# Half-target edge buckets: count matmuls of 314 columns, four plain evacuations on ScalarE, and biases added later

## The reference

```python
u = xn @ root + bias
for r in range(8):
    mask = (edge_type == r)
    sums = segment_sum(xn[src] * mask[:, None], dst, num_segments=625)
    cnt = segment_sum(mask, dst, num_segments=625)
    u = u + (sums / maximum(cnt, 1)[:, None]) @ weight[r]
z = concatenate([u, xn], 1) @ w_gate + b_gate
h = tanh(u) * z + xn * (1 - z)
```

## Time and profile before

| | us |
|---|---|
| median of 3 runs | 1880.09 |
| lowest, highest | 1879.5, 1880.28 |
| profiled execution: span from first to last instruction | 1878.8 |
| PE busy (share of the span) | 1794.9 (96%) |
| DVE busy | 1023.3 (54%) |
| ACT busy | 478.5 (25%) |
| POOL busy | 701.1 (37%) |
| chain that ended last: share of PE | 84% |

### The profile page before, as it was taken

One profiled execution on the slowest core, in us unless ns is written; L12 is line 12 of the kernel. 1 busy time (PEld: TensorE's weight loads), 2 busy tenths in 40 slices (PEclk: granted clock), 3 DMA queues, 4 the chain that ended last, 5 costly groups with the idle time before them and its releaser, 6 DMA issues.

```text
span 1878.8 us, 28666 instructions
## 1 busy us (share of the span) xinstructions
PE 1794.9 (96%) x9953; PEld 1477.4 (79%) x9953; DVE 1023.3 (54%) x2540; ACT 478.5 (25%) x1055; POOL 701.1 (37%) x609
## 2 busy tenths in 40 slices
PE   6999999999999999999999999954999999999999
PEld 4876689987777778787777887742899888878987
DVE  7888999997254543526354356786632224362311
ACT  3139956662010110101011145243100000111100
POOL 2110000003634435353534444200485552345862
PEclk9999999999999999999999999956999999999999
DMA  4532222224213121231313534110354351113322
GB/s 134 154 109 77 73 86 79 75 67 129 91 38 89 45 72 56 66 86 47 94 33 113 172 84 131 45 46 7 96 164 146 104 156 51 37 55 118 90 73 66
DMA packets 129282, 162.23 MB, mean 86 GB/s; under 512 B 14288, under 2 KB 75368, under 8 KB 128922
## 3 DMA queue, kind: packets, MB, share of 16 engines
q1 hardware_dynamic: 100848, 120.93, 21.5%
q10 hardware_dynamic: 22250, 23.53, 4.0%
q0 software_dynamic: 6080, 16.40, 2.9%
HBM read 135.51 MB, written 25.30 MB: 86 GB/s over the span
## 4 chain that ended last, share of the span: by engine, by line
PE 84%; DVE 6%; ACT 6%; issue 1%; DVEq 1%; DMA 1%; POOL 0%; ACTq 0%; SPq 0%
PE ps L367 22%; PE ps L368 22%; PE ps L369 21%; PE ps L1236 9%; PE ps L892 3%; ACT sc_col L838 2%; ACT sc_row L837 1%; PE ps L1201 1%; DVE w_lo L318 1%; PE ps L881 1%; PE ps L1156 1%; DMA nat<-in_x 1%; ACT w_hi L313 1%; PE ps L1183 1%; PE ps L1211 0%
## 5 line engine op out<-in xcount | busy, mean ns | idle before, releaser
L367 PE MATMUL ps<-w_hi,xt_hi 128*125 128x512 f32 x1320 | 539.0, 408 | 9.1 <-DVE xt_lo L549 3.5
L256 POOL TENSOR_TENSOR w_hi<-w_stage,zero 128x512 fp32r<-128x512 f32 x256 | 276.8, 1081 | 684.4 <-PE ps L369 670.0
L368 PE MATMUL ps<-w_lo,xt_hi 128*125 128x512 f32 x1320 | 523.0, 396 | 0.0
L369 PE MATMUL ps<-w_hi,xt_lo 128*125 128x512 f32 x1320 | 521.5, 395 | 0.0
L259 POOL TENSOR_TENSOR w_lo<-w_stage,w_hi 128x512 fp32r<-128x512 f32 x256 | 346.2, 1352 | 20.1
L367 PEld LDWEIGHTS ps<-w_hi,xt_hi 128*125 128x125 f32 x1320 | 246.6, 187 | 67.1 <-DVE xt_lo L549 4.3
L369 PEld LDWEIGHTS ps<-w_hi,xt_lo 128*125 128x125 f32 x1320 | 246.0, 186 | 63.3
L368 PEld LDWEIGHTS ps<-w_lo,xt_hi 128*125 128x125 f32 x1320 | 246.3, 187 | 53.5
L367 PE MATMUL ps<-xt_hi,w_hi 128*128 128x314 f32 x736 | 250.5, 340 | 1.3 <-DVE ring L2430 0.6
L369 PE MATMUL ps<-xt_hi,w_lo 128*128 128x314 f32 x736 | 225.9, 307 | 0.0
L368 PE MATMUL ps<-xt_lo,w_hi 128*128 128x314 f32 x736 | 225.7, 307 | 0.0
(11 more groups left out here) (392 smaller groups left out, 2390.2 us busy)
## 6 DMA issues: line engine op xcount, KB each, us to landing
w_stage<-in_stream SPq DMA_DIRECT2D x374, 256.0 KB, 2.7
pre<-ring POOLq DMA_DIRECT2D x30, 250.0 KB, 3.8
a_qt<-pre_t SPq DMA_DIRECT2D x18, 312.5 KB, 3.8
a_qt<-pre_t ACTq DMA_DIRECT2D x14, 312.5 KB
pre_t<-ring_t POOLq DMA_DIRECT2D x12, 312.5 KB, 2.8
...
```

Of the source, the lines that this page charges most:

```text
L256: POOL.tensor_tensor(w_hi[:, q, :], w_stage[:, q % NST, :], zero[:].to_broadcast([128, 512]), ALU.add).then_inc(S("hi_done"), 1)
L367: PE.matmul(dst, l_hi, r_hi, start=first, stop=False)
L368: PE.matmul(dst, l_hi, r_lo, start=False, stop=False)
L369: return PE.matmul(dst, l_lo, r_hi, start=False, stop=last)
```

## The change

**Buckets.** The key becomes (type x 5 + tile) x 2 + (target is 314 or more): 80 buckets, each padded to whole chunks of 128, again 240 chunks. The column one-hot has 314 columns instead of 626; each chunk's counts are one matmul of 314 columns in a bank of its own, with no sum over two chunks. ACT copies two chunks in one instruction; DVE adds each chunk apart (240 adds of 314). The row one-hots of four chunks are made by one tensor-tensor comparison of 512 elements (`iota1_by4` against four columns of `slot_row`), and PE reads each with a step of four elements. Addresses are ready-made in `g_start` and loaded into four registers at once. The one-hot of chunk c + 4 stands behind the add of chunk c.

**Sorting.** `key_hot` has 28 rows; three fields of 8 bits share a row, with weights 1, 2^8, 2^16, and a scan over 28 x 166 elements counts all 84. `ranks` and `rank_fields` take each edge's rank out of the packed sums; `positions` makes each bucket's start by 80 comparisons with a multiply, in int16, and folds them.

**Evacuations and biases.** Groups 0 to 3 leave PSUM by ACT without bias (`evacuate_plain`). Their biases are loaded by SP (`load_bias_h`) and added by DVE (`bias_half`) to nat, which has relations' u by then, and to z before its first use.

```diff
-GROUP = 256
-NGROUP = (EDGES + NBUCKET * (GROUP - 1)) // GROUP
-NCHUNK = 2 * NGROUP
+SPLIT = 314
+NKEY = 2 * NBUCKET
+FIELDS, NROW = 3, 28
+NFIELD = FIELDS * NROW
+CHUNK = 128
...
+        def evacuate_plain(g):
+            for m in range(T):
+                wait_bank(ALE, g, m, c0, g0)
+                if g:
+                    ALE.wait_ge(S(f"st{tag}_{m}"), 16 * g)
+                ALE.activation(ring[:, m, :], ps[0:P, m, :], ACT.Copy).then_inc(S("bank_free"), 1)
...
         def evacuate(g):
-            DVE.wait_ge(S("b" + tag), 16 * g + 16)
+            DVE.wait_ge(S("b" + tag), 16 * (g - G_PLAIN) + 16)
             for m in range(T):
                 wait_bank(DVE, g, m, c0, g0)
-                if g:
-                    DVE.wait_ge(S(f"st{tag}_{m}"), 16 * g)
+                DVE.wait_ge(S(f"st{tag}_{m}"), 16 * g)
...
+        DVE.tensor_tensor(key_hot[:], e_row[:].unsqueeze(1).to_broadcast([P, NROW, EW]),
+                          iota16[0:P, 0:NROW].unsqueeze(2).to_broadcast([P, NROW, EW]), ALU.is_equal)
+        split_low_dve(8, 11)
+        DVE.drain()
+        DVE.tensor_tensor(key_weight[:], key_hot[:], e_weight[:].unsqueeze(1).to_broadcast([P, NROW, EW]), ALU.mult)
         split_low_dve(11, 16)
...
+        kw = key_weight[:].rearrange("p b c -> p (b c)")
+        DVE.tensor_tensor_scan(scan[:].rearrange("p b c -> p (b c)"), kw, kw, 0.0, ALU.add, ALU.max)
...
+    def ranks():
+        DVE.tensor_tensor(scan[:], scan[:], key_hot[:], ALU.mult)
+        DVE.drain()
+        n = NROW
+        while n % 2 == 0:
+            n //= 2
+            DVE.tensor_tensor(scan[:, 0:n], scan[:, 0:n], scan[:, n:2 * n], ALU.add)
+            DVE.drain()
+        DVE.tensor_reduce(e_rank[:], scan[:, 0:n].rearrange("p b c -> p c b"), AX.X, ALU.add)
+        DVE.drain()
...
+    def positions():
+        for b in range(NKEY):
+            DVE.tensor_scalar(key_start[:, b, :], e_key16[:], float(b), b_off[:, b:b + 1], ALU.is_equal, ALU.mult)
+            if b == NKEY // 2:
+                split_low_dve(24, 27)
         split_low_dve(27, 31)
         DVE.drain()
-        n = NBUCKET
+        n = NKEY
         while n % 2 == 0:
             n //= 2
-            if 2 * n == NBUCKET:
-                h = n // 2
-                DVE.tensor_tensor(scan[:, 0:h], scan[:, 0:h], scan[:, n:n + h], ALU.add)
-                evacuate(2)
-                DVE.tensor_tensor(scan[:, h:n], scan[:, h:n], scan[:, n + h:2 * n], ALU.add)
+            DVE.tensor_tensor(key_start[:, 0:n], key_start[:, 0:n], key_start[:, n:2 * n], ALU.add)
+            if 2 * n == NKEY:
                 split_low_dve(31, 32)
...
-        DVE.tensor_reduce(e_pos[:], scan[:, 0:n].rearrange("p b c -> p c b"), AX.X, ALU.add)
+        DVE.tensor_reduce(e_pos[:], key_start[:, 0:n, 0:EC].rearrange("p b c -> p c b"), AX.X, ALU.add)
+        DVE.drain()
+        DVE.tensor_tensor(e_pos[:], e_pos[:], e_rank[:, 0:EC], ALU.add)
...
+    LEAD_HOT, STARTS = 4, 4
+    def pair_bank(g):
+        return 4 if g % 2 else 6
+    def hist_hot(c):
+        if c % 4 == 0:
+            if c >= 8:
+                DVE.wait_ge(S("hi_pe"), c - 4)
+            DVE.tensor_tensor(hot_row[c // 4 % 2][:], iota1_by4[:],
+                              slot_row[:, c:c + 4].unsqueeze(1).to_broadcast([128, 128, 4]), ALU.is_equal)
+        if c >= 8:
+            DVE.wait_ge(S("hi_pe"), c - 7)
+        DVE.tensor_scalar(hot_col[c % 8][:], iota1_16[:, 0:SPLIT], slot_col[:, bass.ds(c, 1)], None,
+                          ALU.is_equal).then_inc(S("hi_dve"), 1)
+    def hist_copy(g):
+        b = pair_bank(g)
+        ALE.wait_ge(S("hi_pe"), 2 * g + 2)
+        if g >= 4:
+            ALE.wait_ge(S("hi_add"), 2 * g - 6)
+        ALE.activation(counts[g % 4][:], ps[0:P, b:b + 2, 0:SPLIT], ACT.Copy).then_inc(S("hi_main"), 1)
+    def hist_starts(c):
...
+    def hist_add(c, start):
+        DVE.wait_ge(S("hi_main"), c // 2 + 1)
+        if c:
+            DVE.wait_ge(S("hi_add"), c)
+        o = adj[:, bass.ds(start, SPLIT)]
+        DVE.tensor_tensor(o, o, counts[c // 2 % 4][:, c % 2, :], ALU.add).then_inc(S("hi_add"), 1)
+    def hist_pe(g):
+        if g >= 2:
+            PE.wait_ge(S("hi_main"), g - 1)
+        if g == 1:
+            PE.wait_ge(S("bank_free"), (SC0 + SC_GROUPS + 1) * T)
         for j in range(2):
-            q = 2 * gm + j
...
+            c = 2 * g + j
+            PE.wait_ge(S("hi_dve"), c + 1)
+            PE.matmul(ps[0:P, pair_bank(g) + j, 0:SPLIT], hot_row[c // 4 % 2][:, 0:P, c % 4], hot_col[c % 8][:],
+                      start=True, stop=True).then_inc(S("hi_pe"), 1)
...
+        mk = bucket_counts()
         split_low_dve(16, 21)
+        ranks()
         dense(1)
         mk = bucket_sums(mk)
-        evacuate(1)
         split_low_dve(21, 24)
-        mk = group_buckets(mk)
+        rank_fields()
+        mk = chunk_buckets(mk)
         dense(2)
         mk = pack_buckets(mk)
-        positions(evacuate)
+        positions()
         mk = packed_buckets(mk)
         ALE.dma_start(bias_t[:].rearrange("p g b -> p (g b)"), a["bias"][B_PRE0 + 4:B_PRE0 + 8, :].rearrange(
...
-            for c in range((g + 1) * KT, (g + 2) * KT):
+            for c in range((g + 1) * KT, (g + 2) * KT - 1):
                 split_act(c)
-        load_bias(3)
+            evacuate_plain(g)
+            split_act((g + 2) * KT - 1)
         for c in range(C_HAND, C_HAND + 4):
             split_act(c)
         wait(ALE, mk)
-        mk_zero = sig(ALE.activation(adj[:].bitcast(F32), zero[0:P, :].to_broadcast([P, NBUCKET * NB // 2]), ACT.Copy), "act_step")
+        mk_zero = sig(ALE.activation(adj[:].bitcast(F32), zero[0:P, :].to_broadcast([P, NBUCKET * NB // 2 + 1]), ACT.Copy), "act_step")
...
                 DVE.wait_ge(S("sc_pe"), sc_per + EC + 1)
-                DVE.tensor_copy(slot[:, :, 0:NCHUNK], slot_ps.rearrange("p (a c) -> p a c", a=2))
+                DVE.tensor_copy(slot_col[:], slot_ps[:, 0:NCHUNK])
+                DVE.tensor_copy(slot_row[:], slot_ps[:, NCHUNK:2 * NCHUNK])
                 DVE.drain()
-                for n in range(2):
-                    hist_dve_hot(n, n)
+                for c in range(LEAD_HOT):
...
+        starts = dict(enumerate(hist_starts(0)))
         for h in range(HI_GROUPS):
             for n in range(per):
-                g = h * per + n
-                if g + 2 < NGROUP:
-                    hist_dve_hot(g + 2, (g + 2) % 4)
-                if chunk_at(h, n):
-                    split_dve(chunk_at(h, n))
-                if g % 4 == 0:
-                    packed = DVE.value_load(gpack[0:1, g // 4:g // 4 + 1], min_val=0, max_val=2 ** 24 - 1)
-                hist_dve_add(g, g % 4, packed)
+                for c in (2 * (h * per + n), 2 * (h * per + n) + 1):
+                    hist_add(c, starts[c])
+                    if c + LEAD_HOT < NCHUNK:
+                        hist_hot(c + LEAD_HOT)
+                    if c % STARTS == 0 and c + STARTS < NCHUNK:
+                        starts.update(zip(range(c + STARTS, c + 2 * STARTS), hist_starts(c + STARTS)))
...
+    def load_bias_h(row):
+        for g in range(2):
+            r = B_PRE0 + row + g
+            SP.dma_start(bias_h[g][:], a["bias"][r:r + 1, :].rearrange("o (k f) -> o k f", k=4).to_broadcast([P, 4, 128])).then_inc(S("ld_bh"), 16)
...
         if c == C_PROJ + 4:
             SP.dma_start(bias_p[:], a["bias"][B_PROJ0:B_PROJ0 + 2, :].rearrange("(o g) f -> o g f", o=1).to_broadcast(
                 [P, 2, 512])).then_inc(S("ld_bp"), 16)
+            SP.wait_ge(S("a0_C"), REL)
+            load_bias_h(0)
+        if c == C_GATE + 1:
+            SP.wait_ge(S("gsum"), 1)
+            load_bias_h(2)
         if c == C_GATE + 4:
...
+    def bias_half(into, g):
+        into_g = into[:, :, g * 512:(g + 1) * 512].rearrange("p t (k f) -> p t k f", k=4)
+        DVE.tensor_tensor(into_g, into_g, bias_h[g][:].unsqueeze(1).to_broadcast([P, T, 4, 128]), ALU.add)
     newton_after(mk_deg)
     DVE.tensor_copy(dis[:], rs[:])
+    DVE.wait_ge(S("ld_bh"), 32)
+    bias_half(nat, 0)
     for k in range(5, KT):
         feed_dve(k, k)
+        if k == 6:
+            bias_half(nat, 1)
     DVE.wait_ge(S("ld_w"), 32)
...
+    DVE.wait_ge(S("ld_z"), 32)
+    DVE.wait_ge(S("ld_bh"), 64)
+    for g in range(2):
+        bias_half(z, g)
```

253 lines of the change are left out of this document (130 added, 123 removed).

## The result

The changed kernel takes 1885.82 us (median of 6 runs, 1884.37 to 1887.57); the kernel before, run beside it, 1879.99. The ratio is 1.0031, with a 95% interval of 1.0021 to 1.0042: slower by 5.8 us. I had forecast 1878.1, a little faster. The profiled execution took 1885.17, its span is 1883.6 against 1878.8.

What follows compares the result with a forecast made beforehand. TensorE bounds dense sorting groups, ScalarE the scatter, TensorE and nearly VectorE the count stage; the late side chain has no slack. Terms -9.7 - 0.6 + 1.8 + 5.0 + 1.5 = -2.0 gave 1878.1 us, range 1866 to 1890.

Steps and rivals of the forecast that it cites:

- sorting stage: To about 140 us: later low splits delay group 1's bank, ScalarE's clearing delays group 3's evacuation; +1.8 us (0.4 to 4).
- end of the scatter: First one-hots before the evacuation shrink from 1.83 to 1.17 us; -0.6 us.
- count stage: 242 to 429 us: 120 count groups fall from 184 to 174.3 us, paced by a loop over ScalarE's copy; -9.7 us.
- late biases and clock: Near 1132 to 1152 us: late z rows delay the clips, +5.0 us; the pause costs clock, +1.5 us.
- The loop from pair to pair but one: Count stage: matmuls, copy, add, one-hots, matmuls again; 2.75 us for two pairs, 165 us for 120.
- rival B: Count stage: the 512-element one-hot runs at one element a cycle; +13 us, 1891 us; chance 0.2.
- Rival C: Count stage: ScalarE's copy arrives before VectorE is ready, 1.25 to 1.30 us a pair; 1860 us; chance 0.12.
- half of them fall into slack: 9.6: Count stage: of 32 low splits of 0.6 us in VectorE's queue, half are hidden, so they add 9.6 us.
- the clip, due at 1141.02: Late biases: additions to z end at 1146.0, so the weight clip due at 1141.02 is 5.0 us late.
- the list of signs: Signs of a right forecast, among them TensorE idle some 5 us at its second feed beside the projection, about 1140.
- Rival A: Late biases: z rows land early enough and the additions fit into VectorE's idle 8 us; 1871.6 us; chance 0.13.
- rival D: Sorting stage: 80 pointer operations take 0.31 us each, late clearing leaves group 4 no free bank; 1887 us; chance 0.1.

Runs made afterwards that it cites:

- e2: The changed kernel with the one-hots 6 chunks ahead of the additions instead of 4; 1875.91 us, ratio 0.9979 to the kernel before.
- e10: The changed kernel with the count stage's 32 low splits moved from VectorE's queue to GpSimd's; 1897.72 us, ratio 1.0094 to the kernel before.
- e6: The changed kernel without z's bias, its two additions and two row loads left out; 1876.95 us, ratio 0.9981 to the kernel before.
- e7: The changed kernel with the key comparison in halves, low splits between, and group 3's banks emptied by VectorE; 1886.30 us, ratio 1.0031.
- e1: The changed kernel with z's two bias rows issued 5 weight chunks earlier on SyncE's queue; 1887.35 us, ratio 1.0036 to the kernel before.
- e3: The changed kernel with the key comparison cut into halves and the first three low splits between them; 1889.01 us, ratio 1.0050.

## Why the prediction was wrong

The range of 1866 to 1890 held the time, the sign did not: -2.0 was forecast, +4.8 came in the profiled execution. By its terms:

| term | predicted | profile |
|---|---|---|
| sorting stage | +1.8 | +3.25 |
| end of the scatter | -0.6 | -0.5 |
| count stage | -9.7 | -5.2 |
| late biases and clock | +6.5 | +8.9 |
| elsewhere | 0 | -1.6 |

**The count stage's mechanism was right, one term of it was mis-sized.** It holds the largest of the misses, 4.5 us. The loop from pair to pair but one, walked step by step, was to take 2.75 us for two pairs; 28 rounds without a split average 2.72. The one-hot of 512 spaces 0.33 as taken (rival B falls), the addition 0.24 for 0.23. Rival C, a loop under 1.3 us a pair, did not come either. The step that failed is "half of them fall into slack: 9.6" for the 32 low splits. A round with a split takes 3.20, so 0.48 of its 0.60 us lie on the path: 15.4 us; by the medians, 3.24 and 2.64, all of it does. 60 x 2.72 + 15.4 is 178.6, and the start of the stage, before the rounds settle, makes 180.8. My 174.3 left that start out (and is 0.3 under its own terms, 165 + 9.6), but so did the 184 that I took for before, which measures 185.99. There was hardly slack to fall into: with the copy out of the way (e2) a round without a split still takes 2.52. The share of the splits is read from the rounds of one kernel; e10, which was to take them out, added contention instead and can't confirm it. That the loop is what e2 relieves, and VectorE's own sum the next bound 11 us further, the runs show. TensorE's own cost of a pair was right, seen in e2 where nothing is late:

```profile
326.29 0.31 PE L373 MATMUL ps<-xt_hi,w_lo 128*128 128x314 f32 x1
326.43 0.43 PE L977 MATMUL ps<-hot_col,hot_row 128*125 128x314 f16 x2
326.59 0.41 PE L371 MATMUL ps<-xt_hi,w_hi 128*128 128x312 f32 x1
326.84 0.31 PE L372 MATMUL ps<-xt_lo,w_hi 128*128 128x312 f32 x1
```

From 326.43 to 326.84 stand the pair and one dense matmul of 0.145: 0.27 for the pair, as for 43 of 111 pairs from 250 to 405 us (0.26 to 0.28); the others wait. The strided weight load costs nothing bare, as taken. The one-hot of 314 spaces 0.21 at the closest, as the rows of before gave, and not the 0.14 worked out from the Trainium skill (VectorE: DVE Perf Modes, "The TRN2 errata"). Its average of 0.30 in e2 comes from where it stands, between two additions that wait for each other, and was in no term of mine.

**The late biases: right place, right chain, too small.** Lateness was 8.2 us instead of 5.0, of which 7.4 show as TensorE's added wait; the clock took about 1.5 as said. The step that failed is "the clip, due at 1141.02": I measured the lateness in the old times, though the stages before were to gain 8.5 us in my own sum. They gained 3.0, the clips were due at 1138.0, and that is the difference but for 0.2. When the rows landed I had right by luck. I had them issued at 1135.5 and landing 4.9 us later like the weight load beside them, at 1140.5; they were issued near 1132.0 and took 8.6 us, to 1140.6. e6 confirms the whole price (8.9), and e7 shows that the landing follows only in part when the rest comes earlier (0.7 of 2.1 us). The gap stood ahead of TensorE's feed at 1152.75, the one of the sum, and not near 1140, as the list of signs had it. Rival A, that they fit into the idle time, falls with e1: the idle time is long enough, but the rows can't be had in it.

**The sorting stage: right wait, larger.** Bank 0 for group 1 was to be free at 56.6; the last split before it ended at 57.2 and the first matmul started at 57.8. The three loads behind the late splits left at 51.9 to 53.2 instead of 50.8 to 52.0, and landed at 54.6, 55.3 and 56.5. ScalarE waited for the second and the third of them too:

```profile
54.57 0.63 ACT L317 ACTIVATE w_hi<-w_stage 128x512 fp32r<-128x512 f32 x1 [6.31 <-DMA w_stage<-in_stream]
55.35 0.63 ACT L317 ACTIVATE w_hi<-w_stage 128x512 fp32r<-128x512 f32 x1 [0.15 <-DMA w_stage<-in_stream]
56.53 0.63 ACT L317 ACTIVATE w_hi<-w_stage 128x512 fp32r<-128x512 f32 x1 [0.55 <-DMA w_stage<-in_stream]
57.07 2.53 ACT L470 ACTIVATE ring<-ps 125x512 f32<-125x512 f32 x5
```

The end of the bucket work near 128 was right (127.8), and rival D's long pointer operations did not occur: 41 of them take 7.2 us, 0.18 each where I took 0.17. But D's second half, a clearing that holds group 3's evacuation, is real in e3, where the bucket work ends 3 us later and group 1 no longer waits.

**The chances.** 0.3 for slower was too little, for a sum of -2.0 out of a gain of 10 and losses of 8. Both large terms erred to the same side: I took work as hidden (half the splits) where no row showed the slack, and I took a transfer's lateness in old times although my own sum had moved them. That 1885.8 lies in the range is owed to its width of 24 us.
